# Receptance rows turned on VectorE after a round trip through DRAM, and hashed outputs stored in dealt order

## The reference, cut to what matters

```python
# end of layer 0, one expert per batch, chosen by sel
h = gelu(einsum('bsh,bhf->bsf', y, w1[sel]) + b1[sel])
reasoned = einsum('bsf,bfh->bsh', h, w2[sel]) + b2[sel]
x1 = x + y + 0.3 * (reasoned @ Wo + bo)
...
# layer 1, token shift and mix
dx = shifted(x1) - x1
xk = x1 + dx * time_maa_k
xr = x1 + dx * time_maa_r
# xk rows go to one of 16 experts by a hash of the token id, 256 rows each
h = square(relu(einsum('ecd,edf->ecf', expert_in, w_key)))
expert_out = einsum('ecf,efd->ecd', h, w_value)
r = sigmoid(xr @ w_recept.T)
x2 = r * expert_out[slot]
...
# a recurrent scan over the 32 batches follows
```

## Time and profile before

| what | value |
|---|---|
| median of three executions | 2496.48 us |
| the profiled execution's own time | 2494.64 us |
| its span, first to last instruction | 2492.9 us |
| PE busy | 2429.3 us, 97% of the span |
| DVE, ACT, POOL busy | 1195.2, 901.0, 548.4 us |
| feed-forward stage | about 866 to 1465 us |
| hashed stage | about 1465 to 1850 us |
| recurrent stage | about 1850 to 2490 us |
| granted TensorE clock, mean | 0.993 |

### The profile page before, as it was taken

The page is one execution under the profiler, slowest core; times in us unless marked ns, Lnnn a source line. Parts: engine busy times, 40 slices in busy tenths (PEclk is TensorE's granted clock), DMA queues, the critical chain, the costliest instruction groups (busy, mean ns, idle before and its releaser), DMA issues.

```text
span 2492.9 us, 40630 instructions
## 1 busy us (share of the span) xinstructions
PE 2429.3 (97%) x12307; PEld 2021.7 (81%) x12309; DVE 1195.2 (48%) x1833; ACT 901.0 (36%) x1459; POOL 548.4 (22%) x498
## 2 busy tenths in 40 slices
PE   8999999999999899999999989999999999999999
PEld 4778888888899688888888868888888888888877
DVE  5555455325343243443444357777753333333356
ACT  3233333216555322222222236666652222222234
POOL 1100000002222266666666610000001111111100
PEclk9999999999999899999999999999999999999999
DMA  8698888407466533364345256666642111111135
GB/s 287 203 336 301 304 320 312 164 18 275 164 214 248 178 114 115 109 254 120 106 126 178 93 197 223 235 242 225 233 171 77 51 44 45 51 46 46 42 101 185
DMA packets 165172, 420.68 MB, mean 169 GB/s; under 512 B 31379, under 2 KB 67699, under 8 KB 148578
## 3 DMA queue, kind: packets, MB, share of 16 engines
q1 hardware_dynamic: 137810, 322.08, 37.2%
q0 software_dynamic: 19072, 61.66, 8.1%
q10 hardware_dynamic: 8208, 35.88, 3.8%
HBM read 558.71 MB, written 144.80 MB: 282 GB/s over the span
## 4 chain that ended last, share of the span: by engine, by line
PE 68%; DMA 2%; DVE 2%; issue 2%; ACT 1%; SPq 0%; POOL 0%; another core or an unknown queue 0%; DVEq 0%; POOLq 0%; ACTq 0%
PE s_g L99 8%; PE s_g L101 8%; PE s_g L100 8%; PE s_h_ps L99 5%; PE s_h_ps L101 5%; PE s_h_ps L100 5%; PE s_z_ps L99 2%; PE s_z_ps L101 2%; PE s_z_ps L100 2%; PE s_o_ps L99 2%; PE s_o_ps L100 2%; PE s_o_ps L101 1%; PE s_h L99 1%; PE s_h L100 1%; PE s_h L101 1%
## 5 line engine op out<-in xcount | busy, mean ns | idle before, releaser
L99 PE MATMUL s_g<-wx_hi,s_x_hi 128*128 128x512 f32 x512 | 203.3, 397 | 2.3 <-DVE s_x_lo L2339 1.6
L101 PE MATMUL s_g<-wx_hi,s_x_lo 128*128 128x512 f32 x512 | 199.8, 390 | 0.0
L100 PE MATMUL s_g<-wx_lo,s_x_hi 128*128 128x512 f32 x512 | 199.4, 390 | 0.0
L2234 POOL DMA_INDIRECT s_y<-mid_hash_out,first_rec x32 | 31.5, 985 | 736.0 <-DMA mid_hash_out<-s_o 392.7
L2045 DVE TENSOR_TENSOR s_w_lo<-s_w_raw,s_w_hi 128x1024 fp32r<-128x1024 f32 x124 | 146.4, 1221 | 46.6 <-ACT s_w_hi L1974 45.4
L99 PE MATMUL s_h_ps<-s_x_hi,s_w_hi 128*128 128x256 f32 x512 | 145.7, 285 | 7.1 <-DVE s_x_lo L2077 7.1
L99 PE MATMUL s_g<-s_u,s_c_hi 128*128 128x512 f32 x384 | 150.2, 391 | 1.6 <-PEq L1858 1.6
L101 PE MATMUL s_g<-s_u,s_c_lo 128*128 128x512 f32 x384 | 149.9, 390 | 0.0
L100 PE MATMUL s_g<-s_u,s_c_hi 128*128 128x512 f32 x384 | 149.4, 389 | 0.0
L101 PE MATMUL s_h_ps<-s_x_hi,s_w_lo 128*128 128x256 f32 x512 | 145.5, 284 | 0.0
L100 PE MATMUL s_h_ps<-s_x_lo,s_w_hi 128*128 128x256 f32 x512 | 145.5, 284 | 0.0
(11 more groups left out here) (411 smaller groups left out, 6747.3 us busy)
## 6 DMA issues: line engine op xcount, KB each, us to landing
s_half<-mid_w ACTq DMA_DIRECT2D x124, 2048.0 KB
s_w_raw<-in_w SPq DMA_DIRECT2D x64, 512.0 KB, 6.1
mid_w<-s_x_grp SPq DMA_DIRECT2D x32, 1024.0 KB, 5.8
mid_w<-s_pool_b SPq DMA_DIRECT2D x32, 1024.0 KB, 4.9
s_half<-mid_w SPq DMA_DIRECT2D x32, 1024.0 KB
s_w_raw<-in_w2h SPq DMA_DIRECT2D x16, 2048.0 KB, 9.1
s_w_raw<-in_w1h SPq DMA_DIRECT2D x15, 2048.0 KB, 7.5
mid_routed<-s_o_sb SPq DMA_DIRECT2D x72, 256.0 KB
```

The source lines that it names most:

```text
L99: pe.matmul(out, a_hi, w_hi, start=first, stop=False, skip_group_check=True)
L100: pe.matmul(out, a_hi, w_lo, start=False, stop=False, skip_group_check=True)
L101: return pe.matmul(out, a_lo, w_hi, start=False, stop=last, skip_group_check=True)
L2234: pool.indirect_dma_start(y[:], None, d["hash_out"], bass.IndirectOffsetOnAxis(rec[:, SLOTH:SLOTH + 1].bitcast(U32), 0)).then_inc(S["y_in" ...
```

## The change

Three edits.

1. In the feed-forward stage the rows xr of batches 0 to 29 are no longer turned by PE. POOL writes xr in quarter order, SP stores it to a DRAM tile (`mid_xr_rows`) in dealt order and, once that has landed, loads it back by quarters. DVE turns it into an SBUF tile `xrt`, from which ACT makes `xr_hi` and DVE makes `xr_lo`; both stand at the end of the step. Batches 30 and 31 keep the turn on PE.
2. `turn_quarters` now writes the turned tile with unit step: column 32s+t holds row 4t+s. The recurrent stage keeps the old write under the name `turn_dealt_quarters`.
3. The hashed stage uses the new `turn_quarters`, so the rows of its outputs come in that other order, and their store deals them back: partition 32s+t goes to DRAM row 4t+s, a DRAM pattern of 4 x 32 x 512 elements.

```diff
+def dealt(rows):
+    return rows.rearrange("(t s) c -> s t c", s=4)
+def turn_dealt_quarters(dve, dst, src):
+    return dve.transpose(dst.rearrange("p k (t s) -> p k s t", s=4), src.rearrange("p (s k a) -> p k s a", s=4, a=32))
...
 def turn_quarters(dve, dst, src):
-    return dve.transpose(dst.rearrange("p k (t s) -> p k s t", s=4), src.rearrange("p (s k a) -> p k s a", s=4, a=32))
+    return dve.transpose(dst.rearrange("p k (s t) -> p k s t", t=32), src.rearrange("p (s k a) -> p k s a", s=4, a=32))
...
+            def store_xr(i, n, turn):
+                if isinstance(i, int) and i >= NB - 2:
+                    return
+                wait_apart(sp, S["xr"], i + 1)
+                sp.dma_start(dealt(xr_rows[n]), xr[:]).then_inc(S["xr_sent"], 16)
+            def load_xr(i, n, turn):
+                if isinstance(i, int) and i >= NB - 2:
+                    return
+                wait_apart(sp, S["xr_sent"], i * 16 + 16)
+                load_by_quarters(sp, xr[:], xr_rows[n], S["xr_quarters"])
...
-            software_pipeline(sp, NB, [(0, load_rec), (2, load_b2), (1, load_b1), (3, store_x1),
-                                       (0, load_shared), (0, load_x), (5, store_r)], 2)
+            software_pipeline(sp, NB, [(0, load_rec), (4, store_xr), (2, load_b2), (4, load_xr), (1, load_b1),
+                                       (3, store_x1), (0, load_shared), (0, load_x), (5, store_r)], 2)
...
-                    wait_for(pool, S["txr"], i)
-                    pool.tensor_tensor(xr[:], k_part[:], x1[:], ALU.add).then_inc(S["xr"], 1)
+                    wait_for(pool, S["xrt"], i)
+                    if is_next_to_last(i):
+                        pool.tensor_tensor(xr[:], k_part[:], x1[:], ALU.add).then_inc(S["xr"], 1)
+                    else:
+                        pool.tensor_tensor(by_quarter(xr[:]), in_order(k_part[:]), in_order(x1[:]), ALU.add).then_inc(S["xr"], 1)
...
-                (0, load_w2), (1, h_hi(1)), (3, hashed_hi(0, 2)), (4, copy_r), (3, xr_hi_),
-                (3, hashed_hi(2, DC)), (0, y_hi_), (0, load_second)], 2)
+                (0, load_w2), (1, h_hi(1)), (3, hashed_hi(0, 2)), (4, copy_r), (3, late(xr_hi_, True)),
+                (3, hashed_hi(2, DC)), (0, y_hi_), (0, load_second), (3, late(xr_hi_, False))], 2)
...
+            def turn_xr(i, n, turn):
+                if isinstance(i, int) and i >= NB - 2:
+                    return
+                dve.wait_ge(S["xr_quarters"], i * 16 + 16)
+                wait_for(dve, S["xr_lo"], i)
+                turn_quarters(dve, xrt[:], xr[:]).then_inc(S["xrt"], 1)
...
-                (3, xr_lo_), (2, last_mix), (3, hashed_lo(2, DC)), (0, make_shift),
-                (0, y_lo_)], 2)
+                (3, late(xr_lo_, True)), (2, last_mix), (3, hashed_lo(2, DC)), (0, make_shift),
+                (0, y_lo_), (3, turn_xr), (3, late(xr_lo_, False))], 2)
...
-            def turn_xr(sooner):
+            def turn_xr(which):
                 def stage(i, n, turn_no):
-                    if sooner == (isinstance(i, int) and i == NB - 2):
-                        turn(xr, "xr", tz_ps, "z_lo", -2, "txr")(i, n, turn_no)
+                    if isinstance(i, int) and i == which:
+                        pe.wait_ge(S["xr"], i + 1)
+                        pe.wait_ge(S["z_lo"], NB)
+                        for k in range(DC):
+                            mm = pe.transpose(tz_ps[:, k], xr[:, k * P:(k + 1) * P], ident[:])
+                        mm.then_inc(S["txr"], 1)
...
-                (3, turn_xr(False)), (0, turn_y), (1, down)], 2)
+                (3, turn_xr(NB - 1)), (0, turn_y), (1, down)], 2)
...
-                    sp.dma_start(d["hash_out"][bass.ds(e * CAP + m * P, P)], o_sb[m][:]).then_inc(S[f"o_out{m}"], 16)
+                    sp.dma_start(dealt(d["hash_out"][bass.ds(e * CAP + m * P, P)]), o_sb[m][:]).then_inc(S[f"o_out{m}"], 16)
```

More of the change, by code:

```diff
@@ L1378, in stage_ffn @@
         xr = sb("xr", [P, D])
+        xrt = sb("xrt", [P, DC, P])
         xr_hi = sb("xr_hi", [P, DC, P], FP32R)
@@ L1611, in xr_hi_ @@
                 if is_next_to_last(i):
[L1612 removed]
+                    act.wait_ge(S["txr"], 1)
                     act.wait_ge(S["mmo"], NB)
@@ L1615, in xr_hi_, with late, at_end @@
                     return
-                act.wait_ge(S["txr"], i + 1)
-                wait_for(act, S["mmr"], NB - 2 if is_last(i) else i)
-                act.activation(xr_hi[:], tz_ps[:], ACT.Copy).then_inc(S["xr_hi"], 1)
+                if is_last(i):
+                    act.wait_ge(S["txr"], 2)
+                    act.wait_ge(S["mmr"], NB - 2)
+                    act.activation(xr_hi[:], tz_ps[:], ACT.Copy).then_inc(S["xr_hi"], 1)
+                    return
+                act.wait_ge(S["xrt"], i + 1)
+                wait_for(act, S["mmr"], i)
+                act.activation(xr_hi[:], xrt[:], ACT.Copy).then_inc(S["xr_hi"], 1)
+            def late(stage, yes):
+                def at_end(i, n, turn):
+                    if yes == (is_next_to_last(i) or is_last(i)):
+                        stage(i, n, turn)
+                return at_end
             software_pipeline(act, NB, [
                 (2, load_hashed), (2, part_hi(z_hi, tz_ps, "tz", "mmo", 1, "z_hi")), (1, gelu(0)), (0, load_w1), (1, h_hi(0)), (1, gelu(1)),
-                (0, load_w2), (1, h_hi(1)), (3, hashed_hi(0, 2)), (4, copy_r), (3, xr_hi_),
-                (3, hashed_hi(2, DC)), (0, y_hi_), (0, load_second)], 2)
+                (0, load_w2), (1, h_hi(1)), (3, hashed_hi(0, 2)), (4, copy_r), (3, late(xr_hi_, True)),
+                (3, hashed_hi(2, DC)), (0, y_hi_), (0, load_second), (3, late(xr_hi_, False))], 2)
         @block.vector
@@ L1690, in y_lo_, with late, at_end @@
                 part_lo(y_lo, ty_ps, y_hi, "y_hi", "y_lo")(i, n, turn)
+            def turn_xr(i, n, turn):
+                if isinstance(i, int) and i >= NB - 2:
+                    return
+                dve.wait_ge(S["xr_quarters"], i * 16 + 16)
+                wait_for(dve, S["xr_lo"], i)
+                turn_quarters(dve, xrt[:], xr[:]).then_inc(S["xrt"], 1)
             def xr_lo_(i, n, turn):
                 lo, hi = (z_lo, z_hi) if is_next_to_last(i) else (xr_lo, xr_hi)
-                part_lo(lo, tz_ps, hi, "xr_hi", "xr_lo")(i, n, turn)
+                src = tz_ps if is_next_to_last(i) or is_last(i) else xrt
+                part_lo(lo, src, hi, "xr_hi", "xr_lo")(i, n, turn)
+            def late(stage, yes):
+                def at_end(i, n, turn):
+                    if yes == (is_next_to_last(i) or is_last(i)):
+                        stage(i, n, turn)
+                return at_end
             def make_shift(i, n, turn):
@@ L1773, in turn_h, with turn_z @@
                 return stage
[L1775 to L1782, removed]
+            def turn_z(i, n, turn):
+                pe.wait_ge(S["z_add"], i + 1)
+                wait_for(pe, S["z_lo"], i)
+                for k in range(DC):
+                    mm = pe.transpose(tz_ps[:, k], z[:, k * P:(k + 1) * P], ident[:])
+                mm.then_inc(S["tz"], 1)
             def turn_y(i, n, pair):
@@ L1791, in turn_y @@
                     return
-                turn(y, "y", ty_ps, "y_lo", 0, "ty")(i, n, pair)
+                pe.wait_ge(S["y"], i + 1)
+                wait_for(pe, S["y_lo"], i)
+                for k in range(DC):
+                    mm = pe.transpose(ty_ps[:, k], y[:, k * P:(k + 1) * P], ident[:])
+                mm.then_inc(S["ty"], 1)
             def down(i, n, turn):
```

12 lines of the change are left out of this document (7 added, 5 removed).

## The result

The changed kernel takes 2544.98 us (median of four runs, 2543.64 to 2546.27) against 2496.48 before (four runs, 2495.56 to 2496.51): a ratio of 1.0195 [1.0177, 1.0213]. It is slower by 48.5 us. The forecast of 2474.7 and its range of 2469 to 2488 were both wrong, and in the wrong direction.

The account below looks back on a forecast made before the run. The prediction took PE's work plus its few gaps to bound the kernel. Its terms, -13.1 - 10.5 - 0.4 + 2.2 = -21.8 us, took the median of 2496.5 to 2474.7 us, with a range of 2469 to 2488.

Parts of the forecast that it names:

- Part 1: Feed-forward stage: xr's turn leaves PE, 0.44 us off in 29 batches and 0.35 in one, 13.1 us off.
- Nothing in SP's list moves: Feed-forward stage: xr's added store and load fit on SP before b1 must issue at 1039.32, delaying nothing.
- C: Rival, feed-forward gain lost: late quarters or SP held at the landing, PE waits 0.44 a step; 2487.8 us, chance 0.05.
- One or two such steps: Feed-forward stage: heavy steps with late xr that hold SP number one or two, with 6 us of slack in the others.
- Part 2: Hashed stage: unit-step turns bring h_lo 0.77 us sooner; 0.70 off in 15 steps, 10.5 us, plus 0.4 in the first.
- Rival A: Hashed stage keeps its 23.33 us step: turn stays at 1.09 or four engines hold x back; 2485.6 us, chance 0.17.
- Part 3: Hashed stage's dealt stores: four DMA engines, landing 2.2 us later, costing 2.2 us once, at the last store.
- Within the stage nobody waits for these stores: Hashed stage: later landing of dealt stores costs nothing, since each buffer is used again a step later.
- rival B: Hashed stage: four DMA engines become the bound, steps of 25.6 us if the queue runs dry; 2519.6 us, chance 0.08.
- Only the very last does: End of hashed stage: only the last dealt store's landing is waited for, on the chain to PE's turn; 2.2 us on.
- The forecast's sign: Start of the recurrent stage: PE idle about 2 us before L2394 would show the forecast right.
- The end: Last hashed store into the recurrent stage: its later landing adds 2.2 us to the sum.

Follow-up runs that it names:

- e5: Kernel before plus the feed-forward part alone, xr stored plainly and loaded back in four pieces of 32 partitions, wait for the landing kept: 2485.99 us, ratio 0.9966.
- e6: Kernel before plus the feed-forward part alone, store moving a constant tile and load reading rows of x, so no wait for the landing: 2497.87 us, ratio 1.0005.
- e8: Kernel before plus the feed-forward part alone, with plain store of xr, load by quarters kept, turn written with step four: 2491.17 us, ratio 0.9989.
- e3: Kernel before plus the hashed part alone, each dealt store cut into four pieces of 32 rows: 2487.31 us, ratio 0.9969.
- e4: Kernel before plus unit-step turn in the hashed stage, plain stores, loads of x dealt in four pieces of 32 partitions: 2480.91 us, ratio 0.9950.
- e10: Kernel before with only the loads by quarters cut in four pieces of 32 partitions, old turn with step four kept: 2493.65 us, ratio 0.9993.
- e9: Kernel before plus the whole change, with loads in four pieces of 32 partitions and plain stores in both stages: 2475.20 us, ratio 0.9920.

## Why the prediction was wrong

**The gain of the turn leaving PE (Part 1) was real and slightly larger.** Forecast 0.44 a batch; e5, e6 and e8 show 18.78 - 18.28 = 0.50. The change itself got none of it.

**The step that failed first is "Nothing in SP's list moves".** I had checked the new store and load against b1's issue time (1039.32) and against DVE's turn, and found room. I had not followed what stands behind the load in SP's list: `store_x1`, whose copy of shifted rows feeds POOL's dx and so the next xr. Of the two things behind the new wait I had priced one, b1. Three sizes then close the ring, all from the steps at 1063 to 1083 shown above. From the store's issue to the load's pass 5.97 us, where 4.3 was forecast. After the load SP needs 67.59 - 63.82 = 3.8 us until the copy. And dx, r_part and xr take 76.68 - 67.59 = 9.1 from there. With the wait for the landing in SP's list the 6 us of slack at DVE counted for nothing, since the ring doesn't pass through DVE's turn. Slack measured at one consumer is not slack of the loop.

**The second failed step is the price of C.** The mechanism was named ("SP held at the landing") and seen for one heavy step, but its loss was capped at 0.44 a step, what PE had done before for xr. A wait in SP's list delays everything behind it, and such a loss has no cap: in the heavy stretches the store took 17 us and a step 29. "One or two such steps" was not far off in number, but the five around them cost 32 us, not 0.4 each. That the landing, not the traffic, does this is shown for the ordinary steps by e6 (no wait, 18.28) and e5 (wait, short landing, 18.28). For the heavy steps it is not so: e6 shows that few engines beside weight loads cost some 16 us without the wait, and the wait some 18 more. What the sum had wrong is thus Part 1's term: -13.1 forecast, +33.0 measured.

**Part 2, the turn, was right** in its mechanism and a little high in size: the turn takes 0.71 us (the range was 0.62 to 1.09, and I had taken the low end), and e3 and e4 take 0.61 off a step where 0.70 was forecast. e10 shows that the turn did it. Rival A, as a property of the turn, is out.

**Part 3 was mis-sized in place and size.** "Within the stage nobody waits for these stores" holds for their buffers only. Who waits is x, issued behind them and on the same engines: DVE's 18.7 us, of 15 steps. That is rival B, which had 8 in 100. Its break-even of 24.0 us a step was about what came (turn to turn 24.0), so it ate the hashed gain and more; its own step of 25.6 was too long. e3 shows that it was the engines: the same stores in pieces of 32 rows close the wait. The landing of the last store cost 4.0 us instead of 2.2 (6.03 against 2.02), and E grew by 7.5. "Only the very last does" was the third failed step: SP waits for the landing of the last store of `o_0` as well, and PE with it at the end of the stage. The forecast's sign, PE idle about 2 us before its first turn of the recurrent stage, did not come: no idle stands before 1912.09. Along PE, E's growth is +3.0 from the last turn to the last product of the stage (PE waits there 3.2 us for h_lo, where it was 0.9, and 1.7 for the load of c, where it was none), +2.5 idle at the end of the stage and +2.4 for products at the lower clock, less the 0.4 for which PE's second turn no longer waits for its x. The way of the last store is as long: its x for PE's second turn was ready at 1920.56, and PE came to it at 1920.61. In e3, where pieces land soon, PE's side alone makes the 4.2 of 4.3.

**The sum against the runs**, from F, H and E: Part 1 -13.1 forecast, +33.0 came, -10.6 in e5. Parts 2 and 3 in the stage -10.9 forecast, +9.6 came, -11.1 in e4. The end +2.2 forecast, +7.5 came, +0.5 in e4. With the DMAs on all engines the same idea comes near the forecast (2475.2 in e9, from a kernel before that took 2494.9: -19.7 against -21.8), but partly by luck: the turn gives 14 x 0.61 = 8.5 us and not 10.5, and loads that bring x sooner, which the forecast did not have, make up for most of that. The working of PE's and DVE's side held in the main; what failed is that I priced the engine count once, at the last store, and not at every place where a transfer on four engines stands in a list.

Left open: the heavy steps of e5 and e9 (25.05 and 24.86 against 19.8 before) were not brought down, and why the granted clock of the feed-forward stage fell from 1.00 to 0.97 was not tried; it fell where the long steps and PE's idle stretches are (in e5, which has few, it is 1.00 from 866 to 1440), but no run separates the two.

## What to carry to other kernels

When an edit adds a wait to a queue that issues DMAs in a fixed order, write down every issue behind it and follow each to where it meets the wait again: if the sum around that loop is near the step, the loop becomes the bound. Look in the same way for what waits at the end of a stage. In this kernel the transfers whose pattern begins with 4 had a quarter of the DMA engines (shares of 0.25 and 0.29); price such a transfer at every place where it stands, under the heaviest neighbouring traffic, and try it in pieces that begin with 32 (e3, e5) before blaming the idea that it serves.

## What the runs showed of the hardware

- **Landing of 256 KB**: dealt to DRAM on four engines about 5.9 us after issue in ordinary steps and 16.97 beside weight loads; plain, 2.0 in ordinary steps and 10.1 beside weight loads (e5). Both are slower beside weight packets, the one on few engines more so.
- **The pace under weight loads**: in the 16.97 us the packets of the store came at some 16 per us from 1114 to 1119 beside some 17 per us of 16 KB on the weights' queue, and at 50 per us from 1122 to 1123.4, when those had ended (70 packets). The DMA view of the changed kernel from 1106.4 to 1123.4, its total and the shares of two queues (packets, MB, share of 16 engines):

```profile
DMA packets 793, 5.49 MB, mean 323 GB/s; under 512 B 96, under 2 KB 96, under 8 KB 537
...
q10 hardware_dynamic: 288, 4.19, 63.7%
q1 hardware_dynamic: 265, 0.51, 9.2%
```

SP's queue (q1) got 9.2% of the engines' time where the weights' (q10) got 63.7%.
- **An issue can block**: b1's load, normally 0.10 us on SP, took 8.22 and 8.63 in the two stretches of weight loads, and two loads of x 9.88 (6.64 before), in all cases right behind transfers on four engines. In e6, with as many of those, b1 took at most 0.70, but the shifted copies behind it took 5.72 once instead of 1.5; in e5 b1 took at most 0.72. My reading is that the queue was full of unfinished packets; no run tests that by itself.
- **DVE and POOL on SBUF**: with xr_lo made from an SBUF tile instead of PSUM, the same subtraction takes 691 to 1781 ns (median 1176) instead of 681 to 694 in the trace of before. Part 1 had bounded it by 1.3. Its row in the changed kernel (ns min/median/max, first and last start), and the longest of them with what POOL did:

```profile
L1685 DVE TENSOR_TENSOR s_xr_lo<-s_xrt,s_xr_hi x30: 691/1176/1781, 903.1 to 1480.3; 128x512 fp32r<-128x512 f32 x30
...
1283.30 1.78 DVE L1685 TENSOR_TENSOR s_xr_lo<-s_xrt,s_xr_hi 128x512 fp32r<-128x512 f32 x1 [0.70 <-ACT s_xr_hi L1650]
...
1283.25 1.29 POOL L1526 TENSOR_TENSOR s_dx<-s_prev,s_x 128x512 f32<-128x512 f32 x1 [3.88 <-DMA s_prev<-in_cond]
```

In the 25 batches in which a POOL instruction of the mix was running when xr_lo started, xr_lo took 1.03 to 1.78 us, longer the more of that instruction was left; in the 5 others it took 0.69. The other way round, POOL's dx that started just after an xr_lo took 1.81 and 1.84 us instead of 1.29 (1072.12, a link of the ring above, and 1264.27). In e5, with the same tiles at other moments, the median of xr_lo is 0.70.
